# One q projection for all heads, its two f16 parts placed by DMA through DRAM; stages moved by two steps

## The reference

```python
qkv = layer_norm(x, g1, be1) @ w_qkv
q, k, v = ...                                   # each [4096, 8, 16]
scores = einsum('nhd,mhd->hnm', q, k) * 16 ** -0.5
scores = where(adj != 0, scores, -inf)
attn = softmax(scores, axis=-1)
out = einsum('hnm,mhd->nhd', attn, v).reshape(n, 128)
x = x + out @ w_proj + b_proj
h2 = layer_norm(x, g2, be2)
return x + gelu(h2 @ w1 + b1) @ w2 + b2
```

## Time and profile before

| | |
|---|---|
| median of 3 runs | 1792.54 us |
| the profiled execution | 1792.59 us |
| its span in the trace | 1790.8 us |
| TensorE / VectorE / ScalarE / GpSimd busy | 92 / 79 / 74 / 67 % |
| mean granted TensorE clock | 0.97 |
| HBM read / written | 74.33 / 4.19 MB |

### The profile page before, as it was taken

The page is one execution under the profiler, slowest core; times in us unless marked ns, Lnnn a source line. Parts: engine busy times, 40 slices in busy tenths (PEclk is TensorE's granted clock), DMA queues, the critical chain, the costliest instruction groups (busy, mean ns, idle before and its releaser), DMA issues.

```text
span 1790.8 us, 46610 instructions
## 1 busy us (share of the span) xinstructions
PE 1640.1 (92%) x17058; PEld 516.3 (29%) x17058; DVE 1411.1 (79%) x4471; ACT 1322.5 (74%) x1475; POOL 1198.3 (67%) x1129
## 2 busy tenths in 40 slices
PE   6989999999999999999999999999999999999975
PEld 3422222323223232323223232323223232223213
DVE  6888879877898779887898779988799778987501
ACT  4547877787877877787777878777777878778771
POOL 4945587578856777468856788558865788557441
PEclk9869999999999999999999999999999999999995
DMA  7710036202450035301360035301362024400000
GB/s 213 173 42 2 19 107 119 55 1 66 128 110 2 13 101 119 73 1 55 113 121 17 2 97 129 78 2 42 109 106 48 2 77 125 78 2 2 8 7 6
DMA packets 168711, 115.08 MB, mean 64 GB/s; under 512 B 139297, under 2 KB 149026, under 8 KB 168482
## 3 DMA queue, kind: packets, MB, share of 16 engines
q1 hardware_dynamic: 157730, 103.71, 24.2%
q10 hardware_dynamic: 10752, 8.39, 1.6%
HBM read 74.33 MB, written 4.19 MB: 44 GB/s over the span
## 4 chain that ended last, share of the span: by engine, by line
PE 61%; ACT 22%; issue 12%; DVE 2%; DMA 1%; POOL 1%; ACTq 0%; SPq 0%; DVEq 0%; POOLq 0%
ACT probs L738 19%; PE pv_ps L1034 17%; PE ring_ps L971 11%; PE score_ps L1123 11%; PE score_ps L1138 10%; PE score_ps L1057 2%; PE ring_ps L1091 2%; PE score_ps L1047 2%; ACT q_stack L623 2%; PE score_ps L995 2%; PE ring_ps L1082 1%; PE ring_ps L1067 1%; PE ring_ps L1074 1%; ACT halves L714 1%; DVE masked_out L773 1%
## 5 line engine op out<-in xcount | busy, mean ns | idle before, releaser
L773 DVE CUSTOM_DVE_ANT_0 masked_out<-ring_ps,row_mask 128x512 bf16<-128x512 f32 x2048 | 1310.6, 688 | 194.8 <-PE ring_ps L971 159.1
L738 ACT ACTIVATE probs<-score_ps,score_scale 128x1024 f32<-128x1024 f32 x1024 | 1088.0, 1112 | 355.0 <-PE score_ps L1138 346.8
L518 POOL TENSOR_TENSOR probs<-probs,keep 128x1024 int32<-128x1024 int32 x256 | 604.8, 2364 | 314.5 <-ACT probs L738 304.3
L1034 PE MATMUL pv_ps<-probs,v_ones 128*17 128x512 f32 x4096 | 542.4, 602 | 1.8 <-POOL probs L518 0.4
L971 PE MATMUL ring_ps<-k_stack,q_stack 51*64 51x512 f16 x4096 | 490.0, 398 | 13.6 <-DVE row_max L773 12.8
L1138 PE MATMUL score_ps<-q_stack,k_stack 51*64 51x512 f16 x4096 | 372.0, 391 | 32.2 <-ACT probs L738 13.0
L1123 PE MATMUL score_ps<-mask_t,ident_bf 64*64 64x512 bf16 x3072 | 274.8, 387 | 45.9 <-ACT probs L738 17.3
L971 PEld LDWEIGHTS ring_ps<-k_stack,q_stack 51*64 51x64 f16 x4096 | 166.5, 104 | 468.6 <-DVE row_max L773 403.9
L1138 PEld LDWEIGHTS score_ps<-q_stack,k_stack 51*64 51x64 f16 x4096 | 116.6, 104 | 243.5 <-PE score_ps L1123 181.8
L773 DVE DVE_READ_ACCUMULATOR2_ANT row_max<- 128x1 f32 x2048 | 169.7, 83 | 0.0
L1123 PEld LDWEIGHTS score_ps<-mask_t,ident_bf 64*64 64x64 bf16 x3072 | 93.4, 106 | 188.3 <-ACT probs L738 126.6
(11 more groups left out here) (117 smaller groups left out, 897.7 us busy)
## 6 DMA issues: line engine op xcount, KB each, us to landing
adj_in<-adj SPq DMA_DIRECT2D x128, 512.0 KB, 4.1
mask_t<-row_mask SPq DMA_TRANSPOSE x128, 3.8
xq<-xnT_dram ACTq DMA_DIRECT2D x8, 256.0 KB, 2.6
x_res<-x ACTq DMA_DIRECT2D x8, 256.0 KB, 4.1
out<-rows ACTq DMA_DIRECT2D x8, 256.0 KB, 4.6
xnT_dram<-attn ACTq DMA_DIRECT2D x4, 256.0 KB, 4.9
xnT_dram<-halves ACTq DMA_DIRECT2D x4, 256.0 KB, 2.5
w_sb<-L_gnn_w SPq DMA_DIRECT2D x2, 256.0 KB
```

The source lines that it names most:

```text
L518: nc.gpsimd.tensor_tensor(view, view, keep[:, KEPT.index(m), :].unsqueeze(1).broadcast_to([128, 2, TILE]), ALU.mult).then_inc(probs_masked, 1)
L738: nc.scalar.activation(probs[:, (2 * g + n) % SLOTS, :], score_ps[:, half:half + 2, :].rearrange("p a n -> p (a n)"), ACT.Exp, scale=score ...
L773: nc.vector.tensor_tensor_reduce(out=masked_out[:, place % 3, :], in0=ring_ps[:, place % 3, :], in1=row_mask[:, j, ch * 512:(ch + 1) * 512 ...
L1034: last = nc.tensor.matmul(pv_ps[32 * k:32 * k + HD + 1, :], v_ones[:, block_of(g, b), 2 * p + a, :], probs[:, (2 * g + b) % SLOTS, a * TIL ...
```

## The change

One projection with all 128 q columns (`wq_all`) replaces the four; ScalarE makes `q_high` (f16) and `q_x` (f32), GpSimd `q_low = q_x - q_high`. SP stores both to DRAM and loads them from there into the rows of `q_stack`. The rows between, for the shift, are cleared once in one of the two `q_stack`s; they are not written by the loads. The two h2t fills become one with four transposes. The up fills move from steps 19, 21, 23, 25 to 21, 23, 25, 27, down from 30..33 to 31..34, q from 31, 35, 37, 41 to 33.

```diff
-UP_STEPS = [19 + 2 * f for f in range(FC)]
-ACT_FILLS = {16: ("h2t", 0), 17: ("h2t", 1), 31: ("q", 0), 35: ("q", 1), 37: ("q", 2), 41: ("q", 3)}
+UP_STEPS = [21 + 2 * f for f in range(FC)]
+ACT_FILLS = {17: ("h2t",), 33: ("q",)}
-DVE_FILLS.update({30 + s: ("down", s) for s in range(SUB)})
+DVE_FILLS.update({31 + s: ("down", s) for s in range(SUB)})
-Q_ADDS = {g + 1: w[1] for g, w in ACT_FILLS.items() if w[0] == "q"}
+Q_STEP = 34
+Q_STORE_LOAD = 5
-STORE_STEP = 34
+STORE_STEP = 35
@@ sync
+            def store_q(i, par):
+                sp.wait_ge(q_done, i + 1)
+                if i > 0:
+                    sp.wait_ge(q_in, i * (16 * 2 * len(PART_ROW)))
+                for low, part in enumerate((q_high, q_low)):
+                    sp.dma_start(q_dram[1 - par, low], part[:, :]).then_inc(q_stored, 16)
+            def load_q(i, par):
+                sp.wait_ge(q_stored, (i + 1) * 32)
+                settled(sp)
+                for n, first in enumerate(PART_ROW):
+                    heads = q_dram[1 - par, Q_LOW[n]].rearrange("(p a d) n -> a d p n", a=2, d=HD)
+                    for a in range(2):
+                        r = HALF * a + first
+                        sp.dma_start(q_stack[1 - par][r:r + HD, :, :], heads[a]).then_inc(q_in, 16)
...
                     load_adj((i + 1) * SUB + k // ADJ_C, k % ADJ_C, k % 2)
+                    if k == Q_STORE_LOAD:
+                        store_q(i, par)
+                    if k == Q_STORE_LOAD + 1:
+                        load_q(i, par)
@@ gpsimd
-                        nc.gpsimd.tensor_tensor(q_stack[1 - par][:, Q_ADDS[g], :], q_x[:, :], q_neg[:, :], ALU.add)\
-                          .then_inc(q_done, 1)
+                        nc.gpsimd.tensor_tensor(q_low[:, :], q_x[:, :], q_high[:, :], ALU.subtract).then_inc(q_done, 1)
@@ scalar
-                    nc.scalar.activation(q_neg[:, :], bank, ACT.Identity, scale=part_coef[:, 0:1])
+                    nc.scalar.copy(q_high[:, :], bank)
                     nc.scalar.copy(q_x[:, :], bank).then_inc(score_taken, 1)
...
-                    nc.scalar.activation(h2T[:, 256 * what[1]:256 * (what[1] + 1)], bank[:, 0:256], ACT.Identity,
-                                         scale=gb[:, 2:3], bias=gb[:, 3:4]).then_inc(score_taken, 1)
+                    nc.scalar.activation(h2T[:, :], bank, ACT.Identity, scale=gb[:, 2:3],
+                                         bias=gb[:, 3:4]).then_inc(score_taken, 1)
@@ vector
+                nc.vector.tensor_scalar(wq_all[:, :], wqkv[:, 0:DIM], grow[:, 0:1], None, ALU.mult).then_inc(w_rep, 1)
+            for a in range(2):
+                nc.vector.memset(q_stack[1][HALF * a + SHIFT_ROW:HALF * (a + 1), :, :], 0.0).then_inc(q_clear, 1)
             dve.wait_ge(x_first, 16)
@@ tensor
-                    last = nc.tensor.matmul(bank, wq_rep[:, what[1], :], xq[:, :], start=True, stop=True)
+                    last = nc.tensor.matmul(bank, wq_all[:, :], xq[:, :], start=True, stop=True)
...
-                    pe.wait_ge(ln2_applied, (i - 1) * (SUB + 1) + 2 * (what[1] + 1))
-                    for s in range(2):
-                        last = nc.tensor.transpose(bank[:, 128 * s:128 * (s + 1)], rows2[:, 2 * what[1] + s, :], ident[:, :])
+                    pe.wait_ge(ln2_applied, (i - 1) * (SUB + 1) + SUB)
+                    for s in range(SUB):
+                        last = nc.tensor.transpose(bank[:, 128 * s:128 * (s + 1)], rows2[:, s, :], ident[:, :])
...
+                    if ahead == 1 and (g, x) == (STEPS - AHEAD, 0):
+                        pe.wait_ge(q_in, (i + 1) * (16 * 2 * len(PART_ROW)))
```

More of the change, by code:

```diff
@@ L441, in _ @@
         def _(pool):
-            nc.gpsimd.memset(wq_rep[:, :, :], 0.0).then_inc(rep_clear, 1)
+            nc.gpsimd.memset(wq_rep, 0.0).then_inc(rep_clear, 1)
             nc.gpsimd.memset(wk_rep, 0.0).then_inc(rep_clear, 1)
@@ L602, in body @@
                         split_max(i, bcd, g, *SPLITS[g])
-                    if b and g in Q_ADDS:
+                    if b and g == Q_STEP:
                         pool.wait_ge(score_taken, made(SCORES, i, bcd, ACT_PLACE[g - 1]))
                         settled(pool)
-                        nc.gpsimd.tensor_tensor(q_stack[1 - par][:, Q_ADDS[g], :], q_x[:, :], q_neg[:, :], ALU.add)\
-                          .then_inc(q_done, 1)
+                        nc.gpsimd.tensor_tensor(q_low[:, :], q_x[:, :], q_high[:, :], ALU.subtract).then_inc(q_done, 1)
                     if b and g in CONVERTS:
@@ L640, in _ @@
             root(0)
+            act.wait_ge(q_clear, 2)
             act.wait_ge(w_in, 16 * 5)
@@ L680, in take_fill @@
                 if what[0] == "q":
-                    n = i * PAIRS + what[1]
-                    if what[1] == 0 and bcd[2]:
+                    if bcd[2]:
                         act.wait_ge(gelu_done, i * FC)
-                    if not (isinstance(i, int) and i == 0 and what[1] == 0):
-                        act.wait_ge(q_done, n)
-                    nc.scalar.activation(q_neg[:, :], bank, ACT.Identity, scale=part_coef[:, 0:1])
+                        act.wait_ge(q_stored, i * 32)
+                    nc.scalar.copy(q_high[:, :], bank)
                     nc.scalar.copy(q_x[:, :], bank).then_inc(score_taken, 1)
@@ L819, in scale_weights @@
                 dve.wait_ge(rep_clear, 2)
-                for n, rep in enumerate((wq_rep[:, :, :], wk_rep)):
+                for n, rep in enumerate((wq_rep, wk_rep)):
                     heads = rep.rearrange("p q (a r) -> p (q a) r", a=2)
@@ L1044, in act_fill @@
                 if what[0] == "q":
-                    if what[1] == 0:
-                        pe.wait_ge(xq_loaded, (i + 1) * 16)
-                    last = nc.tensor.matmul(bank, wq_rep[:, what[1], :], xq[:, :], start=True, stop=True)
+                    pe.wait_ge(xq_loaded, (i + 1) * 16)
+                    last = nc.tensor.matmul(bank, wq_all[:, :], xq[:, :], start=True, stop=True)
                 elif what[0] == "shift":
```

17 lines of the change are left out of this document (11 added, 6 removed).

## The result

The changed kernel takes 1752.53 us (median of 4 runs, 1750.88 to 1753.59) against 1792.11 (4 runs, 1791.45 to 1794.93) of the kernel before: the ratio is 0.9775, with an interval from 0.9758 to 0.9792. The forecast was 1762, with a range from 1752 to 1774. The profiled execution took 1753.59 us, its span is 1751.4: 39.4 less than before's 1790.8, where the sum had 30.5. As the prediction asked, the q projection is there 14 times. The chain of work that ended last has 58% of TensorE and 5% of GpSimd, instead of 61 and 1.

A forecast was written before the change was run, and what follows sets the result against it. TensorE's own work was taken to bound the kernel, transfers and GpSimd counting only where TensorE waits. Terms: -28.0 q, -5.9 clock, -0.7 h2t, +0.8 last h2t, +2.8 GpSimd, +0.5 start, others 0: -30.5, giving 1762 us, range 1752 to 1774.

The forecast's parts named there:

- Rival A: Whole kernel: the time comes out as the terms sum, 1755 to 1768 us; chance 0.60.
- rival E: More saved than summed, under 1755 us: moved down fill and free place behind step 16 give up to 0.8 a tile; chance 0.07.
- The up fills: Steps 19 to 25 moved to 21 to 27: same number, still odd steps, 0; up to 0.1 us a tile possible.
- h2t: Steps 16 and 17, one fill with four transposes: 0.1 us saved in each of seven tiles, 0.7 (0 to 0.8).
- GpSimd's wait: Head of step 30: TensorE waits 0.7 us for block 27's masking; 0.4 counted in each of seven tiles, +2.8 (0 to 5.6).
- the clock's term: Step 35, tiles 0, 2, 3, 5: dips go with the q fill's wait for ScalarE, 4 x 1.47 = 5.9 us saved.
- The q fills and the clock: Steps 31 to 41: q fills, priced against tile 7 without q, save 4.00 in seven tiles, 28.0 us; clock dips 5.9.
- Down: Fill of step 30 moves to 34, partly covered by ScalarE's copies in both places: 0, plus or minus 4 us.
- Rival C: GpSimd takes over: TensorE waits 2 us more a tile at steps 30 to 43, 14 us go back, 1776; chance 0.14.
- The DMAs: q stores and loads before step 43's row scores: 9.8 us without overlap against 11.8 available, cost 0, 2 us to spare.
- rival D: Late q: loads at a quarter rate land 7.2 us after step 43's row scores, 50 us in all, 1812; chance 0.06.
- rival B: Clock dips follow another wait: 1768 us if all four stay, 1772 with one in each tile; chance 0.13.

The follow-up runs named there:

- no step moved: The changed kernel with up back at steps 19 to 25 and down back at 30 to 33, h2t still one fill: 1754.03 us, ratio 0.9782.
- the two unused places: The changed kernel with two more places reserved in the order of the score banks, at steps 24 and 40, that no fill uses: 1758.24 us, ratio 0.9809.
- the spread kernel: The changed kernel with the four down fills at steps 34, 46, 50 and 52 and the output's store behind the last: 1758.67 us, ratio 0.9809.
- the late loads: The changed kernel with the q store behind adjacency load 8 instead of 5 and the q loads behind load 9: 1796.47 us, ratio 1.0021.
- The start alone: The kernel before with only the changed one's two memsets, additional scaling and their waits: 1792.82 us against 1793.79, ratio 1.0007.
- h2t in two stages: The changed kernel with two h2t fills again, at steps 16 and 17, and a reserved place at step 55: 1754.48 us, ratio 0.9781.
- the split of pair 2: The changed kernel with the second split of maxima of pair 2 alone one GpSimd place later, 28 instead of 27: 1751.71 us, ratio 0.977.
- the conversions alone: The changed kernel with conversions 3 to 9 one GpSimd place later, down fills where the change put them: 1752.93 us, ratio 0.9776.
- both spreads with conversions: The changed kernel with down at 34, 46, 50, 52 and conversions 3 to 9 one place later: 1733.63 us; with pair 2's second split later too: 1731.46.
- up back alone: The changed kernel with up alone back at steps 19 to 25, down staying at 31 to 34: 1755.82 us, ratio 0.979.

## Why the prediction was right and where it was not

The chain was read rightly: GpSimd and the DMAs counted only where TensorE waited, and the kernel went by TensorE's time step by step. Rival A was the mechanism, but the sum was 9 us short, so that the time fell where rival E had it, and of E's two reasons one holds (the free place behind step 16) and one doesn't (the moved down fill).

The step that failed is the pricing of the two stages beside q. The up fills were put at 0 because they "keep their number and stay in odd steps", and gave 3.5; h2t was put at 0.7 by counting transposes, and gave 2.7. These two are 5.5 of the 8.9 us. GpSimd's wait came 0.8 cheaper. The remaining 2.6 lie at the start and the end of the execution, and no run shows that they are the change's. Besides, the clock's term came true for another reason than the one given.

- **The q fills and the clock**: -33.9 forecast, -34.1 measured, by the comparison with no step moved. The control of tile 7 was a sound one. In the three tiles without a dip the q fills gave 4.13, 3.79 and 3.78 (4.00 taken).
- **h2t**: a mis-sized term. The forecast counted the transposes and took the turn of the ring as "some switching". Measured, step 16 gave 0.54, in tile 0 as well, and the two unused places cost as much again at other even steps: what went was a place, at 0.54. Four transposes cost 0.66 instead of 0.88, too. -2.7 instead of -0.7.
- **Up**: the other mis-sized term, and the larger. The forecast had "a gain of up to 0.1 a tile" for leaving step 19. The row to look at was TensorE's own, in the waits of the kernel before: the up products stood 7.2 us in all for ScalarE's exponentials, in 8 waits, seven of them of 1.0 at step 19, as the q fill of step 35 did. An up fill costs 1.52 at step 19, behind ScalarE's copies of the values, and 1.12 at 27. In the changed kernel no up fill waits so, and q has 1.3 in place of 10.2. Of the 3.5, 0.40 in each of seven tiles is this; 0.26 is the unused place at step 19 of tile 0, and the rest is scatter of other steps. The rows of the waits (waiting tile and line, releaser: us, times, longest), before and after:

```profile
PE score_ps L1047 <- ACT probs L738: 10.2, 20, 1.2
...
PE score_ps L1057 <- ACT probs L738: 7.2, 8, 1.0
```

```profile
PE score_ps L1075 <- ACT probs L763: 1.3, 7, 0.4
```

- **Down**: 0 forecast, +0.1 measured: 0.45 at step 30 against 0.47 behind 34. The bounds of 4 either way were too wide.
- **GpSimd's wait at step 30**: 0.7 forecast and 0.71 in the trace; of it 0.27 a tile reach the step (0.4 taken): 2.0 for 2.8. TensorE's waits for GpSimd at the weighing grew from 0.4 to 5.6 us in all, under the 10 that the prediction named. Rival C's pile-up didn't come. It is near, though: the spread kernel met it at step 36.
- **The DMAs and rival D**: right that they cost nothing, with 8.7 us to spare by the trace where the forecast had 2. Its 9.8 us had no term for the landing of the two stores, which is what held the late loads (4.2 us); it did no harm, since adjacency load 6 goes out 15.7 us ahead of the row scores (1431.54 and 1447.26 in tile 6), not 11.8. Six loads of 64 KB into 16 partitions are issued in 2.69 us, and each lands within 3.9, while one of 512 KB took 4.1. The rule of the Trainium skill that the prediction weighed (SBUF — State Buffer, Door 1: The DMA port swizzle) would have the loads at a quarter of the rate and, by an estimate with the rate of the 512 KB row and no overlap, 12.3 us; the trace has at most 6.6 us from the first issue to the last landing. Each takes 2.6 us or more to land and the six go out within 2.69, so they overlap, and what one of them has as its own rate no run here tells. That rival's price was real, as the later loads showed: 43.9 us.
- **The clock**: all four dips went, as forecast, but the reason given ("with the fill at step 35 gone its wait is gone") is not enough, and that the 5.9 came true is in part luck. With the q fill off step 35, dips came at 19 and 37; with the q change and up left at 19, three came at 19 (no step moved) and took back some 4.8 us. The start alone shows that the kernel before has them at 19 and 37 too in some executions. So rival B was right that a dip can come at another fill. The changed kernel has no q fill at 35 or 37 and no up fill at 19, and two of its edits did that together. Its trace and six more without a fill there or a new wait (h2t in two stages, the unused places, the split of pair 2, the conversions alone, both spreads with conversions) show no dip between the start and the last iteration. Since up back alone has the waits at 19 and no dip, these traces don't show by how much the move of up lowers the chance. What starts a dip stays open (the row of step 37 above).
- **The start**: +0.5 forecast; the additions cost nothing that 10 runs can tell.
- **The end**: the serial chain lengthened as worked out: from the last transposes' start to the first up product it is 1728.60 - 1726.65 = 1.95 us against 1.31, 0.64 for 0.8. But the clock rises earlier in that chain: the last down product takes 1.16 us where it took 1.70 before, the third 1.70 for 2.08. The forecast had no term for where the clock stands at the end, and none of the runs was made to settle it.

TensorE's timeline in the last iteration of the changed kernel: h2t, the first up, the last two down products.

```profile
1726.65 1.09 PE L1082 MATMUL score_ps<-ident,rows 128*128 128x128 f32 x4 [10.07 <-POOL rows L594]
1728.60 2.07 PE L1085 MATMUL score_ps<-h2T,w_sb 128*128 128x512 f32 x2 [0.87 <-ACT h2T L716]
...
1744.99 1.70 PE L1119 MATMUL ring_ps<-w_sb,hidden 128*128 128x128 f32 x8 [0.38 <-DVE rows L915]
1747.07 1.16 PE L1119 MATMUL ring_ps<-w_sb,hidden 128*128 128x128 f32 x8 [0.38 <-DVE rows L915]
```

## What to carry to other kernels

Price an inserted piece of work by the step it stands in, from the starts of the pace-setting instruction: here an up or a down fill cost 1.1 us in a step that TensorE sets, an up fill 1.5 behind ScalarE's copies, and a down fill 0.2 to 0.5 in a step that ScalarE sets. Count the ring's places as work of their own: an unused one cost 0.5 us at an even step, and nothing at step 55. And when a change makes the bound engine faster, look next at the fixed order of the engine behind it: the spread of the down fills lost 6 us until one instruction of GpSimd's was taken out of the way, and then gave 19.

## What the hardware showed that was not expected

- A VectorE instruction on 128x4 elements took 2.37 us instead of 0.165 while a GpSimd `tensor_tensor` of 128x1024 ran; in the changed kernel's order the two never met in eight tiles. A GpSimd `tensor_scalar` of 0.6 us made the next such instruction 0.47 us instead of 0.17. The maxima of 128x512, which read PSUM, kept their 0.69 us beside the same GpSimd work.
- The granted clock fell to 0.5 for a stretch, which cost 1.4 to 1.6 us, at fills reached after 0.8 to 1.2 us of waiting for ScalarE (steps 35 and 19) and at one reached after 0.15 us (step 37), in some tiles and not in others with the same lengths; which tiles had it changed from profile to profile. It fell around waits for GpSimd (0.96 and 1.94 us), VectorE (2.28) and the q loads (5.32) too.
- Four 128x128 f32 transposes took 0.66 us, two took 0.44: not in proportion.
- Stores of 128 KB landed 3.7 and 4.2 us after their issue, as late as a load of 512 KB (4.1); the dependent load went out 4.27 us after the second.
